# A graph network on one core: one fp32 product for the edge and the target part, a ring of 32 gathered groups, loads begun by ScalarE

## What is computed

```python
def _mlp(h, W, b, gamma, beta):
    h = relu(h @ W + b)
    mu = mean(h, axis=0); var = mean(square(h - mu), axis=0)
    return gamma * (h - mu) * rsqrt(var + EPS) + beta
...
node_feat = _mlp(x, W_node, ...)
edge_feat = _mlp(edge_attr, W_edge, ...)
message = concatenate([x[row], x[col], edge_feat], axis=1)
message = _mlp(message, W_msg, ...)
agg = segment_sum(message, col)
x = layernorm(x + agg + node_feat)
for l in range(3):                 # attention, softmax over a target's edges
    h = (x @ W[l]).reshape(N, H, C)
    e = leaky_relu(alpha_s[src] + alpha_d[dst])
    ...
    x = relu(segment_sum(h[src] * alpha, dst) + bias[l])
x = layernorm(x0 + x)
```

## Time and profile before

| | us |
|---|---|
| median of 3 executions | 10644.16 (10643.23 to 10644.27) |
| the profiled execution | 10621.61 |
| its span, first to last instruction | 10619.8 |
| busy in the span: PE, PE's weight loads | 6152.5, 5414.6 |
| busy: DVE, ACT, POOL | 4582.6, 3539.3, 6506.8 |
| gathers of the message pass in its block (L790, `table_m`) | 1608.5 in 1603 |

### The profile page before, as it was taken

The page is one execution under the profiler, slowest core; times in us unless marked ns, Lnnn a source line. Parts: engine busy times, 40 slices in busy tenths (PEclk is TensorE's granted clock), DMA queues, the critical chain, the costliest instruction groups (busy, mean ns, idle before and its releaser), DMA issues. The chain is left out here.

```text
span 10619.8 us, 135368 instructions
## 1 busy us (share of the span) xinstructions
PE 6152.5 (58%) x29838; PEld 5414.6 (51%) x29838; DVE 4582.6 (43%) x11874; ACT 3539.3 (33%) x7369; POOL 6506.8 (61%) x6535
## 2 busy tenths in 40 slices
PE   6777777777855555555545555555454555555553
PEld 2366666666644444444444444444444444444443
DVE  8644444444543333333343333333334333333335
ACT  5411111111133333333333333333333333333333
POOL 0166666666656666666656666666665666666665
PEclk6555555555566666666666666666666666666665
DMA  5111111111111111111111111111111111111111
GB/s 140 27 37 37 36 37 37 37 37 37 35 35 34 34 34 34 34 34 35 34 35 34 35 34 35 34 35 34 34 34 36 34 34 34 35 34 35 34 35 29
DMA packets 310442, 395.85 MB, mean 37 GB/s; under 512 B 196635, under 2 KB 204177, under 8 KB 308201
## 3 DMA queue, kind: packets, MB, share of 16 engines
q0 software_dynamic: 206976, 330.75, 15.3%
q1 hardware_dynamic: 101577, 61.83, 2.6%
q10 hardware_dynamic: 1840, 2.78, 0.1%
HBM read 368.10 MB, written 26.82 MB: 37 GB/s over the span
## 5 line engine op out<-in xcount | busy, mean ns | idle before, releaser
L790 POOL DMA_INDIRECT rows<-table_a,idx x4851 | 4797.2, 989 | 2646.5 <-issue 1608.0
L1241 PE MATMUL ps<-ident,work 128*128 128x128 f32 x4872 | 1182.2, 418 | 2613.5 <-issue 2534.5
L1241 PEld LDWEIGHTS ps<-ident,work 128*128 128x128 f32 x4872 | 948.7, 221 | 2700.8 <-issue 2600.7
L1258 PE MATMUL ps<-rows,work 128*128 x9744 | 1759.6, 351 | 943.3 <-ACT work L1190 756.7
L1258 PEld LDWEIGHTS ps<-rows,work 128*128 128x128 f32 x9744 | 1637.2, 261 | 1128.9 <-issue 1125.0
L790 POOL DMA_INDIRECT rows<-table_m,idx x1603 | 1608.5, 1003 | 905.2 <-issue 522.4
L1197 ACT ACTIVATE work<-work,small 128x896 f32<-128x896 f32 x696 | 725.0, 1042 | 3640.9 <-issue 2316.9
L1134 DVE SCALAR_TENSOR_TENSOR work<-dstf,big,select 128x224 f32 x696 | 314.4, 452 | 3163.7 <-SPq L732 1658.0
L1123 DVE CUSTOM_DVE_ANT_0 work<-work,ps 128x896 f32<-128x896 f32 x696 | 757.0, 1088 | 1229.7 <-issue 924.7
L1029 PE MATMUL ps<-W3s,work 97*128 97x96 f32 x3248 | 1015.7, 468 | 349.4 <-DVE work L953 318.6
L1029 PEld LDWEIGHTS ps<-W3s,work 97*128 97x128 f32 x3248 | 909.7, 330 | 522.2 <-issue 274.8
(11 more groups left out here) (256 smaller groups left out, 6042.6 us busy)
## 6 DMA issues: line engine op xcount, KB each, us to landing
rows<-table_a,idx POOLq DMA_INDIRECT x4851
rows<-table_m,idx POOLq DMA_INDIRECT x1617
big<-edge_parts SPq DMA_DIRECT2D x231, 45.5 KB
edge_parts<-big SPq DMA_DIRECT2D x6, 1617.0 KB, 11.7
work<-edge_parts SPq DMA_DIRECT2D x50, 192.0 KB
table_a<-work SPq DMA_DIRECT2D x12, 606.0 KB, 6.4
b_dram<-big SPq DMA_DIRECT2D x3, 1176.0 KB, 8.2
big<-b_dram SPq DMA_DIRECT2D x3, 1176.0 KB
```

The source lines that it names most:

```text
L790: pool.indirect_dma_start(rows[:, k % RING, j, 0:width], None, table, bass.IndirectOffsetOnAxis(ap=idx[:, k // CHUNK, at:at + 1], axis=0)) ...
L1241: last = pe.transpose(ps[:, 4 + j // 4, (j % 4) * P:(j % 4 + 1) * P], prob[:, par, j, :], ident[:])
L1258: last = pe.matmul(ps[:, 6 + par, 0:D + 1], probT[:, par, j, :], rows_of(at("slot", 3))[:, j, 0:D + 1], start=(j == 0), stop=(j == TPG - 1))
```

## The change

**Edge and target part in one product.** `We_dst` (26 rows, 128 columns) holds the edge weights in 96 columns and, in the other 32, the rows of `pick` that give the target's index. One product per half step (L856) writes both, `uT` has 128 partitions: 96 of the relu and 32 of the match, now fp32. `weights` (128 x 96, fp32, two copies) holds the scaled W3 in rows 0 to 95 and in rows 96 to 127 the window's 32 target rows plus `bias_b`. So `message_product` is one fp32 product of 128 rows a tile (L870). The target table stays one fp32 table in DRAM, `table_b`; the three-way split and the stack are gone. The edge products of even and odd steps have banks of their own, and an edge product waits for the match and relu of two steps before it instead of one.

**Loads begun by ACT.** `load_edges` and `load_b` bring edge data and the 32 target rows for a step two ahead, into two buffers each. ACT reads four numbers a pair from the list for that; PE reads none; DVE three quads.

**Ring and pace.** The ring of the message pass has 32 groups of 96 columns (`RING_M`, in `store`), the indices four buffers. All 32 are asked for in the block of the statistics: four at once, and group g > 3 once PE has done 13 (g - 3) chunks. After that group g waits for `freed` and for step 9g/8 - 35 (`PACE_M` = 36 steps for 32 groups).

**Around it.** The node products use seven banks and are made before the end of the statistics' aggregation; the sums of the message pass live in `XT` (cleared by DVE), and POOL writes the row of ones into it behind the message pass. SP waits for each group's gathers and tells `landed`, as before, and no longer loads edge data.

```diff
-ERING = RING
+RING_M = 32
+TOLD_M = 16
+IDX_M = 4
...
+CHUNKS_A_GROUP = 13
...
-LEAD_M = 0
+LAG_M = 28
+PACE_M = RING_M + RING_M // 8
...
-        AHEAD = 2
...
+                pool.wait_ge(s_tab, 16)
+                for g in range(RING_M):
...
+                    if g > 3:
+                        pool.wait_ge(s_u, CHUNKS_A_GROUP * (g - 3))
+                    gather(g, g, 0)
+                def gather_later(i, k):
+                    pool.wait_ge(shared["freed"], i * RING_M + (k - (RING_M - 1)))
+                    pool.wait_ge(m_sems["u_ready"], i * PACE_M + (k + k // 8 + 1 - PACE_M))
+                    gather(None, k, i)
...
+                    for half in range(2):
+                        last = pe.matmul(bank(2 * par + half, P, GE // 2), wt["We_dst"][:],
+                                         edges_in[:, par, half * (GE // 2):(half + 1) * (GE // 2)], start=True, stop=True)
+                    last.then_inc(s["u_ready"], 1)
...
-                            pe.matmul(o, ut[:, j, :], W3s[:], start=True, stop=False)
-                            last = pe.matmul(o, match[:, j, :], b_win[:, par], start=False, stop=True)
+                            last = pe.matmul(ps[:, 4 + half, (j - j0) * D:(j - j0 + 1) * D], both_parts[:, j, :], weights[:, par],
+                                             start=True, stop=True)
...
+                def load_edges(par, column):
+                    act.dma_start(edges_in[:, par, :], edge_parts[:, bass.ds(column, GE)]).then_inc(s_edges[par], 16)
+                def load_b(par, node):
+                    act.dma_start(b_in[:, par, :], table_b[bass.ds(node, WA), :]).then_inc(s_bin[par], 16)
...
-                    dve.tensor_scalar(eqT[:, par].rearrange("p (b n) -> p b n", b=2), ps[0:3 * WA, 0:2, 0:GE // 2],
...
-                    dve.scalar_tensor_tensor(b_win[:, par], b_all[:, bass.ds(at("parts", 0), D)],
+                    dve.tensor_scalar(uT[D:, par].rearrange("p (b n) -> p b n", b=2), ps[D:, 2 * par:2 * par + 2, 0:GE // 2],
+                                      base_w[D:, bass.ds(at("window", 0), 1)], pshift[D:, bass.ds(at("shift", 0), 1)],
                                       ALU.subtract, ALU.is_equal).then_inc(s["eqt_ready"], 1)
+                    dve.wait_ge(s_bin[par], q * 8 + (16 - 8 * par))
+                    dve.tensor_tensor(weights[D:, par], b_in[:, par], bias_b, ALU.add).then_inc(s["win_ready"], 1)
```

More of the change, by code:

```diff
@@ new lines, in gnn_kernel, with listed @@
+        sp_wanted, dve_wanted, pe_wanted = (e.alloc_register(f"wanted{k}") for k, e in enumerate((nc.sync, nc.vector, nc.tensor)))
+        most = PAIRS - 2
+        bounds = dict(row=(0, NWA * ROW_A), ready=(TPG, NG * TPG), window=(0, NWA), table=(0, (WA - 1) * TBW),
+                      slot=(0, (RING - 1) * TPG * TW), slot_m=(0, (RING_M - 1) * TPG * D), edges=(0, EPAD - GE),
+                      node=(0, NPAD), shift=(0, WA - 1))
+        def listed(eng, quads, at_quads, wanted, i):
+            k0, k1 = wanted[0], wanted[-1] + 1
+            _, values = nc.values_load_multi_w_load_instructions(
+                steps[bass.ds(i, 1), at_quads + 4 * k0:at_quads + 4 * k1], engines=[eng.engine], min_val=0, max_val=TOP,
+                skip_runtime_bounds_check_because="the list is made of steps within these bounds")
+            return {e: nc.s_assert_within(v, *bounds[e[0]], skip_runtime_bounds_check_because=
+                                          "the list is made of steps within these bounds")
+                    for e, v in zip(sum(quads[k0:k1], []), values) if e}
@@ new lines, in node_sums, with step @@
+                def node_sums(k, par):
+                    pe.wait_ge(s["rr_ready"], k + 1)
+                    if not (isinstance(k, int) and k < 2):
+                        pe.wait_ge(shared["done"], k - 1)
+                    for j in range(TPG):
+                        last = pe.matmul(ps[0:MW, 6 + par, 0:WA], rr[:, par, j, :], eq[:, par, j, :], start=(j == 0), stop=(j == TPG - 1))
+                    last.then_inc(s["s_ready"], 1)
+                def step(q, par, live, at):
+                    if live(0):
+                        edge_product(q, par)
+                    if live(1):
+                        message_product(q - 1, (par - 1) % 2)
+                    if live(2):
+                        node_sums(q - 2, (par - 2) % 2)
@@ new lines, in _ @@
+                dve.tensor_scalar(lift[:, D:], ones[0:D, 0:WA], small[0:D, 40:41], cols[:, 5:6], ALU.mult, ALU.add).then_inc(s_ew, 1)
+                for par in range(2):
+                    dve.tensor_scalar(weights[0:D, par], wt["W3"][:], small[0:D, 39:40], None, ALU.mult)
+                dve.memset(rr[:, :, :, D:MW], 1.0)
+                dve.memset(square_sums, 0.0)
+                dve.wait_ge(s_c1, 1)
+                dve.tensor_copy(bias_b, ps[D:, 7, 0:D]).then_inc(s_weights_m, 1)
+                dve.wait_ge(s_xin, 16 * 2)
```

679 lines of the change are left out of this document (324 added, 355 removed).

## The result

The changed kernel takes 10534.5 us in the median (10514.08 to 10553.78, four runs) beside 10643.69 for the kernel before (10643.23 to 10644.27, four runs) on the same chip. The ratio is 0.9897, 95% interval 0.9876 to 0.9918: 1.0% faster, where 2.5% was forecast. The profiled execution took 10524.89 us, its span 10523.1.

What follows compares the result with a forecast made beforehand. It took the gather rhythm, 10.70 us a group, as the bound of statistics and message pass: pass end 254 + 225x = 2662 for 2927, 265 us off 10621.6, 10357, plus 22.6 for the median: 10380 us, range 10040 to 10640.

Steps and rivals of the forecast that it cites:

- the rhythm of the gathers sets the end: Statistics and message pass: permissions come each 7.8 and 7.6 us, sooner than 8.75 us a group, so gathers set the time.
- x: Time of a group of seven gathers in statistics and message pass, taken as 10.70 us; pass ends at 254 + 225x.
- rival (4): Message pass: DVE has no slack for stops, 15.2 + 9.5 us for two groups, x = 12.35, 10750 us; chance 0.14, mostly slower.
- main case: Whole kernel: gather rhythm x from 10.3 to 11.2 us, total 10290 to 10490 us; chance 0.45.
- PE's step: Message pass: PE's work a step falls to 6.6 us from 9.2, with fp32 products at 0.45 us each.
- DVE's step: Message pass: DVE's work a step falls from 5.49 to 4.9 us, 13.2 a pair with a 3.4 us load.
- ACT's loads: Message pass: ACT gains two transfers and a four-number load per pair, 1.8 us, staying below 6.75 us a step in all.
- rival (5): Message pass: ACT's loads come late, held up by gathers; each 0.5 us a step is 111 us, about 10490; chance 0.08.
- Node products: Between statistics and message pass: node products, clearing and first load take 30 us, the products themselves 10 us.
- The groups ahead: First 32 groups gathered during the statistics: 27x there until the chunks left, then 198x in the message pass.
- the 265 us: Message pass forecast to end at 2662 us for 2927, so 265 us off the profiled execution's 10621.6.
- What follows the pass: After the message pass: attention stays; clearing at once and the row of ones cost nothing, uncovered some 10 us.

## Why the prediction was wrong

**The step that failed** is "In both stages, then, the rhythm of the gathers sets the end", with x = 10.70 taken from the pass before since its cause "is still there". The cause was there, and what it does was read rightly: stops after a long run, ended some 2.5 us after it. But 10.70 is not a property of the gathers, and a permission came each 7.6 us only as long as nothing stood. The rhythm is the time in which the other engines earn POOL the permission for two more groups, with the stop added. Where that work shrinks the rhythm follows, and where much of it is hand-overs, as in the statistics, all of the stop counts:
- Statistics: 15.6 + 9.7 = 25.3 us for two groups, 12.6 a group for 10.7. 27 groups, 52 us; 66 in all, of which some 7 are the gathers' start, at 107 for 100.
- Message pass: 2.25 x 6.69 = 15.05 us, and 22.1 were measured (two groups at 11.06), so a stop of 7.1. 198 groups, 71 us.
That is the mechanism of rival (4), to which I gave 0.14, with a stop of 7.1 us where I put 9.5 and where 8.6 decided between faster and slower. The 7.1 is what is left of 22.1. DVE's waits between 800 and 2400 us (waited for, us in total, times, longest), before and after, show about as much:

```profile
DVE work L953 <- remote: 359.6, 72, 11.5
DVE big L911 <- remote: 80.6, 27, 5.8
```

```profile
DVE work L1058 <- remote: 209.3, 45, 9.9
DVE XT L1023 <- remote: 186.4, 35, 8.3
```

With the shorter rows of the same two instructions that is 478 us before and 477 after, 6.3 and 6.6 us for two groups. So the 9.5 us came from one pair of steps that was worse than most; the stops hardly grew, and the sum with 6.6 gives 21.7 of the 22.1. The 11.06 of the pass lies within the 10.3 to 11.2 that the forecast allowed x, the 12.6 of the statistics does not. That the kernel still came out faster was luck as far as the forecast goes: its main case put no price on a stop that is added to the engines' work, and one of 8.6 us would have undone the gain. Two runs show the sum: with one group a step it gives 13.4 + 7.1 = 20.5 for two groups, and 21.0 was measured; without stops (a pause behind each gather) the statistics ended at 369.

**Term by term.**
- PE's step: right. L870's fp32 products take 0.50 us for my 0.45 (bounds 0.45 and 0.62), the whole 6.55 for 6.6:

```profile
L870 PE MATMUL ps<-work 128*128 128x96 f32 x3248 | 817.6, 443 | 615.0 <-DVE work L1058 439.8 <-issue 169.6 <-DVE work L1040 5.5
L1036 DVE TENSOR_SCALAR work<-ps,base_w,pshift 32x896 f32<-32x896 f32 x232 | 283.6, 1222 | 424.0 <-issue 353.5 <-PE ps L870 36.3 <-remote 26.8
```

- DVE's step: right. The match 1.22, the addition of 32 x 96 0.24 for 0.25. The load, in rows that answer to the earlier trace rows:

```profile
L548 DVEq TENSOR_LOAD <-steps x6: 1614/1629/1691, 1517.3 to 1612.6; - x6
L548 ACTq TENSOR_LOAD <-steps x6: 670/699/732, 1517.3 to 1612.6; - x6
```

Eleven numbers in 1.63 us, fifteen in 2.15, four in 0.70: 0.13 us each, as the rows of before gave. DVE stood 3.4 us a pair.
- ACT's loads: no wait for them is seen beside the stops; rival (5) did not come.
- Node products: 518.32 to 543.80, 25.5 us for 30. Right.
- The groups ahead: I counted them as a gain of 28 rhythms in the pass and a loss in the statistics of about as much each; the loss was larger, and the median shows nothing of what they were to bring of the 265 us. The 1.0% is that of the rest (the common product, its waits a step later, ACT's loads), as the run with four groups ahead shows with its ratio of 0.9899; these were not run apart.
- What follows the pass: costed at nothing, "uncovered some 10 us". It took 35 us more in the profiled execution, in two parts. From the last addition to the first gather of attention it was 81 us for 69. Rows of DVE and POOL there:

```profile
2803.89 8.90 DVE L1444 TENSOR_SCALAR lift<-ident,small 96x96 f32<-96x96 f32 x1
```

```profile
2796.12 16.60 POOL L1493 MEMSET store<- 128x19800 f32 x1 [66.66 <-POOLq L714]
```

A DVE instruction of 96 x 96 takes 8.90 us and ends at 2812.79, when POOL's clearing ends, at 2812.72. Before, the clearing was in two parts, the first of 11.34 us from 2928.08 on, and the same instruction took 4.28 and ended with it:

```profile
2935.20 4.28 DVE L1422 TENSOR_SCALAR lift<-ident,small 96x96 f32<-96x96 f32 x1
```

So clearing at once cost 4.6 us on the path. Here the trace agrees with the rule of the Trainium skill that did not fit the gathers (page "SBUF — State Buffer", Who interferes with whom: the loser of the shared port pair waits for the other's instruction). The rest of the 12 us lies in the folding of the sums, beside a lower clock of PE: there the granted clock was 0.96 before (near the upper level, 2.4 GHz) and 0.50 after (the lower, 1.2 GHz), and a round of its three products took 4.2 us for 2.2. First the row of before, then that of after; PE is busy 95% and 100%.

```profile
2950.00:2972.00 22.00, 20.82 (x169) 19.56 (x169) 20.69 (x111) 18.74 (x51) 1.83 (x1) 0.96 0.30 59
```

```profile
2822.00:2860.00 38.00, 38.00 (x181) 37.66 (x182) 25.16 (x126) 24.48 (x65) 4.35 (x9) 0.50 0.18 33
```

Why it rose before and not after was not tried, and that the clock costs the rest is read from these rows, not run. The other 22 us lie in attention, which the change hardly touches; the four runs of the changed kernel spread over 40 us, and this stays open.

**The choice among the cases.** The forecast let the stop vanish in the engines' slack, and only rival (4) added it to their work; the rows of the statistics already showed chunk after chunk waiting in a stop.

## What to carry to other kernels

When a rhythm of before is carried over to a changed loop, ask what it is the sum of: here the others' work for a permission plus the stop, so that gathers moved into another stage brought the stop with them and gained nothing in the median. Take the price of a stop from a whole stage, not from one pair of steps. Where long runs of gathers stop other engines, try to slow them: writing 370 columns of zeros behind each gather freed the statistics wholly, 1300 behind seven only in part. In the whole kernel the second was better all the same (0.971, and 0.962 with attention, for 0.978 in one execution), since the first made POOL the bound of the pass. Time both kinds of chip before choosing: where nothing stops, the pause behind each gather took the changed kernel from 0.970 to 1.019 of the kernel before.

## What the runs showed of the hardware

Chips of the same kind differed in this by a sixth of the kernel's time: 10644 us with stops, 8964 without, from the same program. Each was met for one or two short series only, so whether this belongs to the chip, or to something beside it at the time, is not known. On the first, gathers 1.25 us apart held up the hand-overs of PE, ACT and DVE after some 11 us; with zeros written between them, 1.53 to 1.59 us apart, never in the statistics and the pass. On the second they ran 1617 in a row, 9.03 us a group, and nothing stopped. Neither POOL's being busy (zeros in their place) nor the bytes (a quarter of each row) decides it. The place of the cause, whether it is the rate or the break that counts, and the rate at which stops begin, stay open.
